# A convolution, attention and expert block: five groups in flight, and f32 expert tiles in halves of the array

## The reference

```python
x = x + _L0_conv_ref(_gn(x), ...)      # group norm over channel pairs; 3x3 depthwise conv with softmax over an axis of 1: all taps are 1; + bias + input
t = _to_tokens(x)
t = t + _L1_attn_ref(_ln_t(t), ...)    # layer norm; queries; 4 hashes x 8 buckets (argmax of rotated tokens)
                                       # tokens averaged by bucket -> 32 keys and values per image; 8-head attention
                                       # + residual; layer norm; fc1, gelu, fc2; + residual
t = t + _L1_ffn_ref(_ln_t(t), ...)     # router, top 2 of 8 experts; h = silu(x w1) * (x w3), 682 wide; y = h w2; gated sum
```

## Time and profile before

| | us |
|---|---|
| median of 3 runs | 996.07 (993.58 to 1000.67) |
| profiled execution, span | 1006.2 |
| PE busy in it | 718.8 (71%) |
| DVE busy | 662.4 (66%) |
| POOL busy | 518.7 (52%) |
| ACT busy | 482.1 (48%) |

### The profile page before, as it was taken

How to read it: one execution, slowest core, us unless ns; L and a number is a source line. 1 busy time by engine, 2 the same in 40 slices (tenths; PEclk the granted TensorE clock), 3 DMA queues, 4 the chain that set the end, 5 groups by cost and what they waited for, 6 DMA issues and landing times.

```text
span 1006.2 us, 22282 instructions
## 1 busy us (share of the span) xinstructions
PE 718.8 (71%) x5921; PEld 548.8 (55%) x5922; DVE 662.4 (66%) x1518; ACT 482.1 (48%) x859; POOL 518.7 (52%) x603
## 2 busy tenths in 40 slices
PE   0277868688586885867943208999999999999943
PEld 0265757567375674654823106666666666667622
DVE  0357777585675856747562536887888787888854
ACT  0013535234253342523331107778878787888741
POOL 4114052543826438254353464776767676767650
PEclk9858857556575575755555559999999999999975
DMA  0010100101001010010100020111111111111018
GB/s 22 10 32 1 32 1 15 32 17 32 11 15 32 16 32 11 6 29 8 33 11 11 13 50 19 29 27 24 25 24 27 26 26 26 24 26 26 23 41 215
DMA packets 57421, 27.26 MB, mean 27 GB/s; under 512 B 46432, under 2 KB 52800, under 8 KB 57392
## 3 DMA queue, kind: packets, MB, share of 16 engines
q1 hardware_dynamic: 45488, 15.99, 6.9%
q0 software_dynamic: 8640, 8.54, 3.0%
q10 hardware_dynamic: 3264, 2.37, 0.7%
HBM read 15.64 MB, written 11.68 MB: 27 GB/s over the span
## 4 chain that ended last, share of the span: by engine, by line
issue 28%; PE 25%; DVE 18%; POOL 17%; ACT 6%; DMA 3%; SPq 1%; another core or an unknown queue 1%; POOLq 1%; ACTq 0%; DVEq 0%
PE bk L994 11%; POOL expert_rows L676 7%; PE bk L1013 4%; POOL expert_results L713 3%; ACT ssub L1192 2%; ACT hbuf L1199 2%; DMA res<-expert_results 2%; PE bk L782 2%; POOL rc L638 2%; POOL hbuf L721 1%; PE bk L1015 1%; POOL r L632 1%; POOL r L628 1%; PE bk L770 1%; PE bk L896 1%
## 5 line engine op out<-in xcount | busy, mean ns | idle before, releaser
L994 PE MATMUL bk<-onehot,w 128*128 128x256 f16 x1704 | 249.0, 280 | 19.7 <-ACT ssub L1192 9.2
L994 PEld LDWEIGHTS bk<-onehot,w 128*128 x1704 | 160.8, 96 | 82.7 <-issue 38.3
L713 POOL DMA_INDIRECT expert_results<-att,dest x142 | 160.0, 1127 | 34.3 <-issue 34.0
L1192 ACT ACTIVATE ssub<-bk,tile_back 128x512 f32<-128x512 f32 x213 | 145.3, 682 | 43.5 <-PE bk L994 40.2
L676 POOL DMA_INDIRECT expert_rows<-srow,pos x128 | 135.5, 1059 | 49.4 <-issue 41.9
L1690 DVE SCALAR_TENSOR_TENSOR prob<-bk,tile_back,ssub 128x512 f32<-128x512 f32 x142 | 106.6, 751 | 58.4 <-ACT ssub L1192 51.8
L721 POOL TENSOR_TENSOR hbuf<-prob,hbuf 128x512 f16<-128x512 f32 x71 | 82.1, 1156 | 79.8 <-ACT hbuf L1199 78.2
L1013 PE MATMUL bk<-w2s,hbuf 128*128 x852 | 102.8, 222 | 7.2 <-POOL hbuf L721 5.7
L1015 PE MATMUL bk<-w2s,hbuf 128*128 x852 | 95.4, 193 | 0.0
L1199 ACT ACTIVATE hbuf<-prob 128x512 f16<-128x512 f32 x142 | 88.9, 626 | 8.4 <-DVE prob L1690 6.6
L1013 PEld LDWEIGHTS bk<-w2s,hbuf 128*128 128x128 f16 x852 | 72.5, 97 | 36.4 <-issue 18.7
(11 more groups left out here) (283 smaller groups left out, 1468.0 us busy)
## 6 DMA issues: line engine op xcount, KB each, us to landing
xin<-expert_rows SPq DMA_DIRECT2D x72, 66.0 KB
res<-expert_results SPq DMA_DIRECT2D x16, 256.0 KB, 3.7
wn<-in_L_ffn_w SPq DMA_DIRECT2D x16, 160.0 KB
expert_results<-att,dest POOLq DMA_INDIRECT x142
xg<-in_x SPq DMA_DIRECT2D x8, 256.0 KB, 2.7
expert_rows<-srow,pos POOLq DMA_INDIRECT x128
out<-og ACTq DMA_DIRECT2D x8, 256.0 KB, 3.5
w2n<-in_L_ffn_w SPq DMA_DIRECT2D x8, 170.5 KB
```

The lines of the kernel that those rows point to most:

```text
L713: g.indirect_dma_start(results[:, :], bass.IndirectOffsetOnAxis(ap=dest[:, b, h:h + 1], axis=0), yout[:, b, h, :], None, bounds_check=DUMP ...
L994: last = mm(bank[:, m, ch * MT:(ch + 1) * MT], w13[:, ds(e, 1), w, 2 * q + ch, part, :].rearrange("p o n -> p (o n)"), xs[:, b, :], start= ...
L1192: f(silu[:, m, :], bk12[:, m, :], ACT.Silu, scale=back).then_inc(silu_ready, 1)
```

## The change

The kernel is written anew around the same three stages; the sizes of groups and expert tiles stay. All arithmetic is f32 now; f16 parts and scales are gone.

**Layout of inputs.** Constants, small weights and the experts' weights reach the kernel packed: w1 and w3 transposed, w1 in partitions 0 to 63 and w3 in 64 to 127, w2 beside them. The output leaves as tokens. The preparation of weights in the group stage, and the transposes and copies of the output stage, are no longer in the kernel.

**Group stage.** Five groups are in flight (`pipeline` has stages a to e), all passes are written out, without loops, and each engine has a new order. ACT takes over the normalising of x (`normalise_x`, `add_x`), the key blocks (`key_blocks`) and the copies of the rows to scatter (`copy_rows`). Each of the three layer norms has buffers of its own. The 16 scatters are split in 5 and 11, in two passes. x has two buffers. Rows are 130 values wide, each token twice. fc1 and the router run as matmuls with 64 rows, one half of the tokens in each half of the array.

**Expert stage.** The weights of each tile (128 x 1,152 f32, 590 KB) are loaded by SP, three tiles ahead, in four buffers; rows in eight. `up` is 12 matmuls of 256 f32 columns: w1 in rows 0 to 63 of the array, w3 in rows 64 to 127, into different banks. `down` is 6 matmuls with 64 output columns each, even and odd chunks in the two column halves; two transposes bring the result back to rows.

```diff
-            def up(t, b, e, between):
...
-                        for ch in range(2):
-                            for part in range(2):
-                                last = mm(bank[:, m, ch * MT:(ch + 1) * MT],
-                                          w13[:, ds(e, 1), w, 2 * q + ch, part, :].rearrange("p o n -> p (o n)"),
-                                          xs[:, b, :], start=part == 0, stop=part == 1)
...
+            def up(t, q):
                 if q == 0:
...
+                    pe.wait_ge(xs_ready, t + 1)
+                    pe.wait_ge(w_loaded[t % W_SLOTS], 16 * (t // W_SLOTS + 1))
+                wait(pe, unit_ready, NU * (t - 1) + q + 1)
+                for ch in range(2):
+                    at = (2 * q + ch) * P
+                    for half, bank in ((0, h1_ps[q]), (1, h3_ps[q])):
+                        part = slice(half * C, (half + 1) * C)
+                        last = mm(bank[:, ch * MT:(ch + 1) * MT], wbuf[part, t % W_SLOTS, at:at + P],
+                                  xs[part, t % 2, :], start=True, stop=True)
+                        if ch == 1:
+                            last.then_inc((h1_ready, h3_ready)[half], 1)
+
+            def down(t):
+                wait(pe, yout_ready, t - 1)
+                pe.wait_ge(unit_ready, NU * (t + 1))
+                for q in range(NU):
+                    for ch in range(2):
+                        at = W2_AT + (2 * q + ch) * C
+                        last = mm(yt_banks[t % 2][ch * C:(ch + 1) * C, 0:MT], wbuf[:, t % W_SLOTS, at:at + C],
+                                  units[:, t % 2, q, ch * MT:(ch + 1) * MT], start=q == 0, stop=q == NU - 1)
+                last.then_inc(down_done, 1)
...
+            turn_rows(0)
+            for t in range(NT):
+                for q in range(NU):
+                    up(t, q)
+                if t + 1 < NT:
+                    turn_rows(t + 1)
+                if t > 1:
+                    turn_results(t - 2)
+                if t > 0:
+                    down(t - 1)
```

The loads of SP, the order of POOL and that of ACT in the group stage, and the pipeline:

```diff
+            def load_weights(t):
+                wait(sp, down_done, t - W_SLOTS + 1)
+                expert = sp.value_load(tile_expert[t:t + 1, 0:1], min_val=0, max_val=NE - 1)
+                sp.dma_start(wbuf[:, t % W_SLOTS, :], weights[ds(expert, 1)].rearrange("e p n -> (e p) n"))\
+                    .then_inc(w_loaded[t % W_SLOTS], 16)
+
+            def load_rows(t):
+                wait(sp, y_scattered[t % X_SLOTS], 32 * (t // X_SLOTS))
...
+            def iteration(a=None, b=None, c=None, d=None, e=None):
+                run(a, group_rstd)
+                run(c, residual)
+                run(c, rstd2)
+                run(e, scatter, 5, 11)
+                run(a, token_rstd)
+                run(d, row_destinations)
+                run(d, scatter, 0, 5)
+                run(c, rstd3)
+                run(a, token_sum)
+                run(a, unit_sum)
...
+                run(c, store_queries)
+                run(b, normalise_x)
+                run(e, router_exp)
+                run(c, repeat_pooled)
+                run(b, add_x)
+                run(c, key_blocks)
+                run(e, copy_rows)
+                run(c, exponentials, 0)
+                run(d, store_n2t)
+                run(b, store_tokens)
+                run(c, exponentials, 1)
+                run(d, gelus, 0)
+                run(c, store_prob, 0)
+                run(b, squares1)
+                run(c, store_prob, 1)
+                run(d, gelus, 1)
...
+def pipeline(iteration):
+
+    for i in range(NG + 4):
+        stages = dict(a=i, b=i - 1, c=i - 2, d=i - 3, e=i - 4)
+        iteration(**{k: n for k, n in stages.items() if 0 <= n < NG})
```

More of the change, by code:

```diff
@@ L66, with places_of, hybrid_block @@
 F32 = mybir.dt.float32
[L67 removed]
 U32 = mybir.dt.uint32
[L69 removed]
 AX = mybir.AxisListType
[L73 to L74 removed]
+CONSTS = dict(ident=P, pair_mean=P, before=P, ones=P, descend=BUCKETS, head_of=HEADS, v_mask=2 * C,
+              v_heads=2 * HEADS, region=NE * NJ, scan_keep=NE * (NJ + 1), k_rows=T // MT, tile_no=1, tile_at=1,
+              pad=2 * ROW, q_one=1, k_one=1)
+SMALLS = dict(bias2=1, g1=1, b1=1, g2=1, b2=1, fc1_bias0=2, proj=C + M + 2 * C, fc1=DFF, fc2=2 * C, fc2_bias=C,
+              router=NE)
+def places_of(table):
+    at, n = {}, 0
+    for name, wide in table.items():
+        at[name] = (n, n + wide)
+        n += wide
+    return at, n
+CONST_AT, NCONST = places_of(CONSTS)
+SMALL_AT, NSMALL = places_of(SMALLS)
+def hybrid_block(nc, x, consts, smalls, weights, out):
     with ExitStack() as ctx:
@@ L927, in iteration @@
-            def iteration(a=None, b=None, c=None, d=None):
-                run(d, router)
+                mm(pos_ps, before, picked[:, :, 1:NJ + 1], start=True, stop=False)
+                mm(pos_ps, ones, passed[:, :, 0:NJ], start=False, stop=True).then_inc(pos_counted, 1)
+            def iteration(a=None, b=None, c=None, d=None, e=None):
+                run(c, attend, 2)
+                run(c, attend, 3)
+                run(b, turn_n1, 1)
                 run(a, pair_means)
                 run(b, rotate)
+                run(a, pair_variances)
+                run(d, turn_wtok)
@@ L942, in iteration @@
                 run(b, scores, 1)
+                run(d, places)
                 run(a, convolution, 1)
-                run(c, fc2)
+                run(c, fc1, 0)
                 run(b, scores, 2)
                 run(b, turn_prob, 0)
+                run(b, scores, 3)
                 run(b, turn_prob, 1)
+                run(c, fc1, 1)
+                run(b, attend, 0)
                 run(b, attend, 1)
-                run(b, attend, 0)
-                run(b, scores, 3)
+                run(c, fc2)
@@ new lines, in _ @@
+            for t in range(NT):
+                for q in range(NU):
+                    n = NU * t + q
+                    act.wait_ge(h1_ready, n + 1)
+                    wait(act, unit_ready, n - NU + 1)
+                    f(silu[:, q, :], h1_ps[q], ACT.Silu).then_inc(silu_ready, 1)
+                if t + 1 < NT:
+                    store_xs(t + 1)
+                if t > 0:
+                    store_results(t - 1)
+            store_results(NT - 1)
+            for b in range(X_SLOTS):
+                act.wait_ge(y_scattered[b], 32 * ((NT - b + X_SLOTS - 1) // X_SLOTS))
@@ L1250, in _ @@
+            for b in range(4):
+                act.wait_ge(out_stored[b], 16 * (NG // 4))
         @block.vector
```

1681 lines of the change are left out of this document (656 added, 1025 removed).

## The result

| | before | after |
|---|---|---|
| median of four runs, us | 995.08 | 811.18 (810.59 to 812.54) |
| ratio, with its 95% interval | 1 | 0.8138 (0.8108 to 0.8169) |
| profiled execution, span, us | 1006.2 | 809.8 |
| group stage with setup, us | 602.6 | 436.1 |
| expert stage, us | 371.6 | 351.4 |

A forecast was written before the change was run, and what follows sets the result against it. No engine fills the group stage, where PE is slow and idle; PE bounds the expert stage. Group stage with setup 443.5, experts 345 and output 28 sum to 816.5 us profiled, times 0.99 gives 808; 8-in-10 range 730 to 940.

The forecast's parts named there:

- The pass: Group stage: a full pass takes 43 us for 62.3, near the 42 that PE needs at the present mix.
- the present mix: Group stage: PE's mean granted clock of 0.61, at which its need was put at 42 of 46 us a pass.
- Rival 1: Group stage: the pass goes warm, 37 us, as PE no longer stops for 3 us; 765 us in total; chance 0.17.
- Terms of other engines: Group stage, busy time a full pass: DVE about 31 us, POOL 34, ACT some 24.
- Fill and drain: Group stage: first passes 25, 34, 40 us; after the full ones 42 and 30, then 18.5 and 26.
- Expert tile: Expert stage: PE bounds each tile at 4.75 us, bounds 4.3 and 7.4; the stage takes 345 us for 371.6.
- Row halves: Expert tile, up projection: matmuls in the two row halves overlap, 2.58 us a tile, 5.16 if not.
- rival 4: Expert tile: row halves go one after another, +2.58 us a tile, 183 in all; total 1000 or 990 us; chance 0.05.
- rival 3: Expert tile: row halves overlap only in part, up projection 3.9 us, +92 us; total of 900 us; chance 0.10.
- Shape changes: Expert tile: three changes between array shapes cost PE 0.14 us each, 0.42 a tile.
- Weights: Expert stage: 0.79 MB a tile moves in 2.9 us at 270 GB/s, covered by PE's 4.75 us.
- Output: Output stage: 28 us for 32.0, as packets grow from 256 B to 2 KB and the bytes stay.

The follow-up runs named there:

- shapes_mixed: Kernel after, with the last tile's down matmuls in three pieces between this tile's up steps, seven shape changes a tile instead of three: 883.03 us.
- weights_near_twice: Kernel after, with SP loading 1,024 of each tile's 1,152 weight columns a second time into unused buffers and PE waiting for both: 826.4 us.
- variances_first: Kernel after, with the next group's channel variances ahead of the product wtok on DVE: 839.63 us, and 838.69 on another chip beside an unchanged control at 844.45.
- down_by_half: Kernel after, with the six down matmuls ordered by column half, three then three, instead of alternating: 842.65 us.

## Why the prediction was right, point by point

**Sum.** 816.5 forecast in the profiled execution, 809.8 measured. Terms: group stage 443.5 and 436.1; expert stage 345 and 351.4; output 28 and 22.3. The step from 816.5 to 808 supposed that the median lies 1% under the profiled span, as before; after, it is 811.18, 0.2% over the span of 809.8. So the expert tile was understood, while the closeness of the total, 3 us, owes much to luck: this factor, the pass, and fill against drain each hide an error that another offsets.

**The pass.** Forecast 43 us, measured 41.1: right in size, wrong in its parts. The prediction let PE's busy time fall from 46 to 42 us at clock 0.61, that is 28.0 to 25.6 at full clock; it fell to 27.5 (level by level, from 28.4 to 28.2). So the f32 forms seem to cost what the weight transposes gave back; the two were not measured apart. In turn the clock, left at "the present mix", rose to 0.75. The two errors offset each other; at 0.61 the pass would have been 45 us of PE's work alone. The step that failed is the claim that 43 stood near PE's need at the present mix. The forecast did say that more than 13.6 us of a pass would run at full clock; it was about 20.5. Rival 1 (37 us, warm throughout) had the direction of the clock, but at 190.7 the clock fell with no stop of PE over 0.68 us in the 12 us before, which neither case allowed for. It also puts in doubt the prediction's reading of the earlier trace rows, that PE's 2.79 us of idle time brought the fall before; why the mean clock rose from 0.61 to 0.75 is open.

**Terms of other engines.** In the three full passes (third window of the stages) DVE has 30.8 us a pass for 31, ACT 22.0 for 24, POOL 29.2 and 16 times 0.3 of issue, 34.0 for 34. None of them fills 41.4 us.

**Fill and drain.** Statistics of the fourth group at 98.5 for 112: the first passes took 17.4, 33.3 and 36.8 us for 25, 34 and 40. From the end of the full passes (304.3) to the first rows of experts 131.8 us for 116.5: the emptying passes and the last group's small steps were priced without the clock, which stood at half from 317 to 440 (0.55 in the window above). These cancel as well: 13.5 us less to the fourth statistics and 9.2 less in the five full passes (205.8 for 215), 15.3 more behind them.

**Expert tile.** 4.81 us for 4.75. Row halves: the two starts of a pair are 7 ns apart, 0.216 us a pair for 0.215 forecast, and undoing it costs 2.59 for the 2.58 of rival 4. The partial overlap of rival 3, with the Trainium skill's 3.07x for four row tiles behind it ("TensorE: Matmul & The Clock Gate", Part 3), falls: for two halves of 256 f32 columns the trace has the full factor of two. Shape changes: 0.14 forecast, 0.18 in shapes_mixed. ACT and DVE stay under PE (24.5 and 28.4 of 48.1 us). L747 takes 2.79 us of a tile from start to start, forecast "about 2.8".

**Weights.** The cover that the prediction named, PE's 4.75 us, holds, and weights_near_twice shows how far: nearly twice the bytes cost 15 us.

**Output.** Forecast from rate and packet size, 28; it moved the bytes at 282 GB/s for 197, so 22.3. Part of this, and of PE's shrinking list, is layout work that left the kernel: the output now leaves as tokens, and the weights come in transposed.

## What to carry to other kernels

Multiply an engine's busy time by its granted clock before comparing kernels: here the work of PE in a pass was 27.5 to 28.3 us in every version without filler, and nearly all of the gain of a pass lay in PE's idle time and its clock. Look at an engine's waits one by one too: they show what an edit did to a chain when the clock blurs the total, and whether a wait went or moved. Matmuls of 64 contraction rows or 64 output columns are worth pairing in the two halves, alternating in the queue, with few changes between shapes. Put a control on the same chip beside edits worth a few per cent: on another chip the unchanged kernel was 4.1% slower, and variances_first, 28 us over the 811.18 of the result, was 6 us under its control.

## What the runs showed of the hardware

- The clock granted to one and the same program differed between two chips: from the fourth to the eighth statistics 0.75 on one and 0.71 on the other, in stretches at full clock of 20.5 us and of 3 to 10 us. The runs do not tell the chip from the hour.
- The clock fell with PE 95% busy before (19.32 of 20.30 us) and stayed at half with PE 95% busy (41.96 of 44.20).
- Matmuls in the two row halves start 7 ns apart at 0.216 us a pair, and the same 24 instructions in one row half take 5.45 us for 2.86.
- By the two trains of starts, a matmul for the other column half started ahead of three of the first half that the code puts before it (down_by_half).
- DVE beside POOL: the product `wtok` of 128 x 512 took 1.78 us, and a product of 128 x 2 (L1005) took 1.03; POOL ran its own 128 x 512 sums at the time. With no sum on POOL beside them they took 0.68 (the row below, from the drain) and 0.16. The Trainium skill ("SBUF — State Buffer", SBUF: two separate sides) says that DVE operations with two inputs in SBUF and POOL operations that read SBUF hold a shared pair of ports in turn, each for its whole length. The trace agrees: `wtok` began 0.05 us behind the 1.28 us of L467 and ended 0.55 us behind it, and L1005 ended with POOL's L473, at 196.5.

```profile
364.60 0.68 DVE L1136 TENSOR_TENSOR wtok<-cent,r 128x512 f32<-128x512 f32 x1
```
